# Graph attention on one core: the scores of a group's four graphs as one run over six PSUM banks, and new issue orders

## What is computed

```python
h = relu(layernorm(x))                      # over the last axis, eps 1e-5
q, k, v = h @ Wq + bq, h @ Wk + bk, h @ Wv + bv      # split into 6 heads of 64
scores = q @ k.T / sqrt(64)                 # per graph and head, 128 x 128
probs = softmax(scores + where(adj, 0, -9e15))
out = x + (concat_heads(probs @ v) @ Wf + bf)
```

## Time and profile before

| | |
|---|---|
| median of 3 runs | 470.05 us (470.0 to 470.82) |
| span of the profiled execution, first to last instruction | 468.2 us |
| own time of the profiled execution | not recorded beside the span; the median of the runs is 1.85 us above the span |
| PE busy | 459.1 us (98%) |
| DVE, ACT, POOL busy | 365.0, 361.6, 303.1 us |
| granted TensorE clock | 1.00 in every slice (the 2.4 GHz level) |

### The profile page before, as it was taken

One profiled execution on the slowest core, in us unless ns is written; L12 is line 12 of the kernel. 1 busy time (PEld: TensorE's weight loads), 2 busy tenths in 40 slices (PEclk: granted clock), 3 DMA queues, 4 the chain that ended last, 5 costly groups with the idle time before them and its releaser, 6 DMA issues.

```text
span 468.2 us, 12877 instructions
## 1 busy us (share of the span) xinstructions
PE 459.1 (98%) x4457; PEld 272.9 (58%) x4457; DVE 365.0 (78%) x742; ACT 361.6 (77%) x816; POOL 303.1 (65%) x308
## 2 busy tenths in 40 slices
PE   6999999999999999999999999999999999999986
PEld 2755656566575665646556575655656565555654
DVE  6989889849988695877869687687877957796855
ACT  3889999865987778877788787688877879687670
POOL 3378578683876765666857577368577648564574
PEclk9999999999999999999999999999999999999999
DMA  8156789879889796986959586969997787788797
GB/s 302 65 121 131 151 130 192 204 141 199 202 141 234 120 212 134 198 194 128 226 111 229 124 177 133 183 146 156 199 182 146 177 170 157 182 139 149 136 158 233
DMA packets 219615, 78.56 MB, mean 168 GB/s; under 512 B 199472, under 2 KB 219568, under 8 KB 219568
## 3 DMA queue, kind: packets, MB, share of 16 engines
q1 hardware_dynamic: 209200, 65.63, 71.5%
q10 hardware_dynamic: 10368, 12.33, 9.9%
HBM read 16.19 MB, written 12.58 MB: 61 GB/s over the span
## 4 chain that ended last, share of the span: by engine, by line
PE 88%; DVE 4%; DMA 3%; ACT 2%; SPq 1%; POOL 1%; issue 1%; ACTq 0%
PE ps_proj L1013 25%; PE ps_proj L1015 24%; PE ps_proj L1014 24%; PE ps_scores L1078 7%; PE ps_ctx L1013 2%; PE ps_ctx L1014 2%; PE ps_ctx L1015 2%; DMA ct_parts<-ctx_parts 1%; DMA pt_parts<-probs_parts 1%; DVE stats L822 1%; SPq L577 1%; ACT probs L757 1%; DMA x_sb<-in_x 1%; DVE w_rows L926 1%; ACT h_pairs L730 1%
## 5 line engine op out<-in xcount | busy, mean ns | idle before, releaser
L657 POOL TENSOR_TENSOR probs_parts<-probs,probs_parts 128x768 f16<-128x768 f32 x64 | 105.2, 1648 | 39.9 <-ACT probs_parts L772 39.8
L757 ACT ACTIVATE probs<-masked,neg_max 128x128 f32<-128x128 f32 x384 | 118.2, 389 | 14.4 <-DVE neg_max L885 8.2
L1015 PE MATMUL ps_proj<-ht_parts,w_lo 128*128 128x512 f16 (+1 forms) x309 | 109.6, 360 | 0.0
L1014 PE MATMUL ps_proj<-ht_parts,w_hi 128*128 128x512 f16 (+1 forms) x309 | 109.6, 360 | 0.0
L1013 PE MATMUL ps_proj<-ht_parts,w_hi 128*128 128x512 f16 (+1 forms) x309 | 109.6, 360 | 0.0
L857 DVE SCALAR_TENSOR_TENSOR qkt_lo<-ps_proj,bias_qk,qkt_hi 128x512 f16<-128x512 f32 x94 | 68.5, 742 | 27.8 <-ACT qkt_hi L741 27.8
L741 ACT ACTIVATE qkt_hi<-ps_proj,bias_qk 128x512 f16<-128x512 f32 x94 | 62.7, 679 | 34.2 <-PE ps_proj L1015 33.9
L663 POOL TENSOR_TENSOR ctx_parts<-ctx_sb,ctx_parts 128x384 f16<-128x384 f32 x62 | 56.7, 918 | 49.9 <-ACT ctx_parts L778 49.9
L876 DVE SCALAR_TENSOR_TENSOR masked<-ps_scores,score_unscale,mask 128x384 f32<-128x384 f32 x128 | 72.0, 609 | 10.3 <-PE ps_scores L1078 9.5
L642 POOL TENSOR_TENSOR h_pairs<-h_sb,h_pairs 128x384 f16<-128x384 f32 x60 | 54.3, 916 | 37.1 <-ACT h_sb L732 36.9
L652 POOL TENSOR_TENSOR x_bf<-x_sb,b_out 128x384 f32<-128x384 f32 x64 | 63.1, 1001 | 9.6 <-DVE y_sb L908 8.1
(11 more groups left out here) (113 smaller groups left out, 916.6 us busy)
## 6 DMA issues: line engine op xcount, KB each, us to landing
x_sb<-in_x ACTq DMA_DIRECT2D x56, 192.0 KB, 3.0
y<-y_sb SPq DMA_DIRECT2D x56, 192.0 KB, 2.5
x_sb<-in_x SPq DMA_DIRECT2D x8, 192.0 KB, 5.1
y<-x_bf SPq DMA_DIRECT2D x8, 192.0 KB, 3.3
pt_parts<-probs_parts SPq DMA_TRANSPOSE x64, 4.0
ct_parts<-ctx_parts SPq DMA_TRANSPOSE x62, 2.8
adj_sb<-in_adj ACTq DMA_DIRECT2D x14, 64.0 KB, 3.6
w_raw<-in_Wk SPq DMA_DIRECT2D x1, 576.0 KB, 5.1
```

Of the source, the lines that this page charges most:

```text
L657: nc.gpsimd.tensor_tensor(probs_parts[b][:, 1, :], probs[b % 2][:], probs_parts[b][:, 0, :], ALU.subtract).then_inc(probs_split, 1)
L757: last = nc.scalar.activation(probs[b % 2][:, u * N:(u + 1) * N], masked[b % 2][:, u, :], ACT.Exp, bias=neg_max[b % 2][:, u:u + 1])
L1014: nc.tensor.matmul(to, a_hi, b_lo, start=False, stop=False)
L1015: return nc.tensor.matmul(to, a_lo, b_hi, start=False, stop=last)
```

## The change

- One PSUM tensor of eight banks without owners. Scores use banks 0 to 5 and `project_qk` the same six, in the order 0, 3, 1, 4, 2, 5; `project_v`, `weigh_values` and `project_out` use banks 6 and 7 (with exceptions in groups 0, 2, 13, 14 and 15). A table `USES_BEFORE` finds for each use who used the bank before, and PE waits for that reader.
- `scores` has three parts of four slots (24 matmuls each) in place of two runs; all four graphs' scores fit at once. A part frees its two banks when the graph after it has been masked: part 0 when `mask_scores(g,1)` is done.
- `masked`, `neg_max` and `probs` have four buffers; the exponentials are written over `masked`.
- All turns are new.

```diff
+BANK = {
+    "project_qk": (0, 3, 1, 4, 2, 5), "project_v": (6, 7, 6, 7), "project_out": (6, 7, 6, 7),
+    "weigh_values": (6, 7, 6, 7),
+}
...
+SCORE_PARTS = SCORE_BANKS // HALVES
+SCORE_SLOTS = B * K // SCORE_PARTS
+LAST_PART = (0, 1, 2, 2)
...
             def exponentials(g, b, i):
                 act.wait_ge(max_ready, nth(B, g, b, i))
-                if g >= 1 or b >= 2:
-                    act.wait_ge(probs_split, nth(B, g, b - 2, i))
                 for u in range(HEADS):
-                    last = nc.scalar.activation(probs[b % 2][:, u * N:(u + 1) * N], masked[b % 2][:, u, :], ACT.Exp,
-                                                bias=neg_max[b % 2][:, u:u + 1])
+                    last = nc.scalar.activation(masked[b][:, u, :], masked[b][:, u, :], ACT.Exp,
+                                                bias=neg_max[b][:, u:u + 1])
...
             def mask_scores(g, b, i):
-                dve.wait_ge(scores_ready, nth(2, g, b // 2, i))
+                dve.wait_ge(scores_ready, nth(SCORE_PARTS, g, LAST_PART[b], i))
...
             def free_bank(stage, group, item, i):
-                before = bank_before(stage, group, item)
-                if before is not None:
-                    was, of, at = before
+                for was, of, at in USES_BEFORE[stage, group, item]:
...
+                    if was == "weigh_values":
+                        pe.wait_ge(ctx_normalized, nth(B, of, at, i))
+                    if was == "scores":
+                        pe.wait_ge(scores_masked, nth(B, of, at + 1, i))
...
-            def scores(g, pair, i):
-                if pair == 0:
+            def scores(g, part, i):
+                if part == 0:
                     pe.wait_ge(qk_split, nth(QK, g, QK - 1, i))
-                if g == 0 and pair == 0:
-                    pe.wait_ge(v_split, 1)
-                if g >= 1 or pair >= 1:
-                    pe.wait_ge(scores_masked, nth(B, g, 2 * pair - 1, i))
+                free_bank("scores", g, part, i)
                 hi, lo = qkt_hi[g % 2], qkt_lo[g % 2]
-                for n, heads in enumerate(SCORE_PAIRS):
-                    if n == MIDDLE_BY_UPPER:
-                        pe.wait_ge(lower_done, nth(2, g, pair, i))
+                for n in range(SCORE_SLOTS):
```

More of the change, by code:

```diff
@@ L44 @@
 TURNS = {
[L45 to L62, removed]
+    "scores": (0, 10, 20), "project_v": (30, 60, 70, 90), "project_out": (10130, 10150, 10190, 20040),
@@ new lines @@
+    "project_qk": (-9950, -9920, -9890, -9860, -9830, -9820), "weigh_values": (160, 200, 10100, 10120),
+    "mask_scores": (0, 30, 40, 90), "normalize_ctx": (250, 10010, 10180, 10200), "largest_score": (20, 70, 80, 120),
+    "finish": (10230, 10240, 10310, 20050), "values_lo": (60, 100, 110, 160),
+    "statistics": (-29730, -29680, -19870, -19850), "additive_mask": (-19860,),
+    "qk_lo": (-9830, -9790, -9740, -9720, -9710, -9700), "aggregate": (-19810,), "shift": (-19780,),
+    "exponentials": (0, 60, 110, 160), "load": (-29790, -29720, -19990, -19930),
@@ L66 @@
     0: {
[L67 to L72, removed]
@@ L187 @@
[L187 to L190 removed]
+        "project_qk": (-9950, -9930, -9900, -9870, -9830, -9820), "project_v": (-9750, -9740, -9710, -9700),
+        "scores": (-9790, -9780, -9770), "weigh_values": (-9620, -9550, -9510, -9460),
@@ new lines @@
+        "project_out": (-9450, -9410, -9390, -9340), "qk_lo": (-9860, -9760, -9750, -9740, -9730, -9720),
+        "values_lo": (-9610, -9600, -9550, -9530), "mask_scores": (-9690, -9680, -9640, -9630),
+        "largest_score": (-9670, -9650, -9620, -9450), "normalize_ctx": (-9430, -9340, -9250, -9170),
+        "finish": (-9140, -9070, -9030, -9000), "qk_hi": (-9940, -9820, -9760, -9750, -9740, -9730),
+        "values_hi": (-9650, -9640, -9610, -9590), "exponentials": (-9710, -9700, -9620, -9430),
@@ new lines @@
+        "project_v": (-39170, -39120, -39110, -38960), "scores": (-39160, -39150, -39140),
+        "weigh_values": (-39020, -39000, -38930, -38880), "project_out": (-38890, -38840, -38830, -38790),
+        "statistics": (-39230, -39220, -39210, -39200), "aggregate": (-39180,), "additive_mask": (-38890,),
+        "qk_lo": (-38810, -38800, -38770, -38740, -38730, -38720), "shift": (-39110,),
+        "values_lo": (-38700, -38630, -38620, -38430), "mask_scores": (-38690, -38660, -38640, -38600),
@@ new lines @@
+        "project_v": (-48910, -48870, -48860, -48810), "scores": (-48970, -48940, -48920),
+        "weigh_values": (-48850, -48820, -48800, -48770), "project_out": (-48760, -48740, -48730, -48720),
+        "turn_ctx": (-48780, -48750), "statistics": (-48960, -48950, -48910, -48900), "aggregate": (-48860,),
+        "additive_mask": (-48750,), "qk_lo": (-48580, -48550, -48540, -48530, -48490, -48470), "shift": (-48840,),
+        "values_lo": (-48330, -48300, -48250, -48240), "mask_scores": (-48450, -48410, -48380, -48360),
```

479 lines of the change are left out of this document (247 added, 232 removed).

## The result

The changed kernel takes **495.12 us** (median of 4 runs, 493.62 to 496.5) against 470.44: ratio 1.0519, 95% interval 1.0491 to 1.0547, 24.7 us slower. The profiled execution took 496.5 us with a span of 494.5. I had forecast 474.7, range 467.0 to 480.5: the side is right, the size is not.

What follows compares the result with a forecast made beforehand. PE, busy 98% of the span, was taken as the bound: 468.2 - 2.3 - 1.6 + 3.6 + 1.9 + 2.6 + 0.5 = 472.9 us of span; with 1.85 from span to median, 474.7 us, range 467.0 to 480.5.

Steps and rivals of the forecast that it cites:

- no other place at which PE would wait by more than 0.2: Groups other than the priced loop starts and groups 3, 10 and 12: no further PE wait above 0.2 us.
- One run of scores, 2.3 less: Edges of score runs on PE: 20 runs instead of 32, each saving 0.19 us of gaps, 2.3 us less.
- rival E: Waits ahead of each score part empty PE's array: 48 gaps in place of 20, 5.3 us more; chance 0.06.
- Banks and buffers, 0: Extra semaphore waits for banks and the exponentials' dropped buffer wait: 0 us; from above 10 us, thought far off.
- The end, 1.6 less: After the last project_qk: PE's waits with lost overlap fall from 2.6 to 1.0 us, 1.6 us less.
- The loop, 3.6 more: Starts of groups 5 to 10: late x loads stall PE on bank 0, 0.6 us six times, 3.6 us more.
- L = 2.9: Assumed landing time in us of a load of x, bounds 2.3 to 3.5; PE stalls L - 2.3 per loop start.
- Group 10, 1.9; group 3, 2.6; group 12, 0.5: Late loads delay values_lo in these three groups, so PE stalls: 1.9, 2.6 and 0.5 us more.
- The period in the loop, 28.4: Time per group in the loop: 28.0 - 0.2 + 0.6 = 28.4 us, with statistics waiting for x_sb some 8 times.
- The start, 0 within 0.5: Start of the kernel: same chain through the weights, reordered, 0 us, ends -0.5 and +0.5.
- Rival D, thin margins, 0.06: DVE's margins of 0.3 to 0.5 us ahead of PE in the loop fail: 5.5 us more, 480 us; chance 0.06.
- The Trainium skill: DMA rule, 2.0 us fixed plus bytes at 436 GB/s: 192 KB load 2.45 us, stalls 3.3, time 469.4 us.

Runs made afterwards that it cites:

- all loads early: Changed kernel with 24 of ACT's entries moved, only loads of x and the mask, each to about where its buffer comes free: 482.2 us, ratio 1.0251.
- one load earlier: Changed kernel with load(G+2,1) moved from behind qk_hi(G,5) to ahead of the group's last normalize: 488.57 us, ratio 1.0399.
- the head's entries alone: Changed kernel with 17 entries of ACT and DVE moved, ahead of or around the first scores: 494.92 us.
- fillers in the changed kernel: Changed kernel with the last block of filler matmuls moved behind turn_first(0,0) and raised from 3 to 10: 491.81 us, ratio 1.0444.
- two experiments: Changed kernel with loads of x and mask moved earlier, 482.2 us; changed kernel with loads of x into a spare tile, DVE not waiting, 482.76 us.
- lists redone: Changed kernel with PE's list kept and 420 entries of the lists of ACT, DVE, POOL and SP moved: 474.67 us, ratio 1.0071.

## Why the prediction was wrong

**The step that failed** is "I went through the other groups in the same way and found no other place at which PE would wait by more than 0.2", and with it "At the start I see the same chain through the weights, reordered: 0". The changed kernel's timeline has 14 more gaps of 0.4 to 2.5 us between 60 and 465 us, 13.9 us together, and 3.7 us in the head. Against the forecast span of 472.9, the measured 494.5 is 21.6 more, and the terms add up to 22.1: 13.9 at places that I had put at nothing, 3.7 in the head, 4.0 more than forecast at the starts in the loop, about 1 by which the waits behind 465 us shrank less than forecast, minus 0.5 at the three places that I had named. I had traced loads to the waits of DVE right behind them and stopped there. One example of how waits go on, ACT and then PE, ahead of `scores(4)`:

```profile
127.43 0.71 ACT L749 ACTIVATE h_pairs<-x_sb,shift_by,rstd 128x384 f16<-128x384 f32 x1 [4.44 <-DVE shift_by L855]
...
130.41 1.61 ACTq L734 DMA_DIRECT2D x_sb<-in_x  x1
132.07 1.27 ACT L760 ACTIVATE qkt_hi<-ps,bias_qk 128x512 f16<-128x512 f32 x2 [1.17 <-issue]
```

```profile
138.28 0.23 PE L1102 MATMUL ps<-qkt_hi 64*128 64x128 f16 x2 [2.03 <-DVE qkt_lo L874]
```

The late mask of group 5 holds DVE for 1.9 us ahead of the statistics, `shift` comes behind these, and `normalize(5,0)` waits 4.4 us on ACT, with `load(6,0)`, `load(6,1)` and `qk_hi(4,2)` to `(4,5)` behind it; the scores need the last of these. The late transfer has a part in a wait of PE two engines further on, in another group's work. It isn't the whole of this one. With the mask early ACT still waits 3.5 us there (the run with all loads early). And of the 2.0 us of PE's wait above, 1.3 belong to this one execution: the start of a load took 1.61 us on ACT's queue in place of 0.34, and ACT idled 1.2 us. In the runs with one load earlier, with the head's entries alone and with fillers in the changed kernel, whose lists are the same at this place, PE waited 0.7 to 0.8 us:

```profile
137.43 0.23 PE L1107 MATMUL ps<-qkt_hi 64*128 64x128 f16 x2 [0.75 <-DVE qkt_lo L879]
```

Point by point:

- *One run of scores, 2.3 less.* Right: the gaps at the scores' edges sum to 6.1 us before and to 3.7 after, and none lies between parts (rival E is out). In the loop, with its load early, PE loses 0.9 against 2.1 before.
- *Banks and buffers, 0.* Right for the buffers (measured 0). For the banks no wait is seen that a set semaphore makes.
- *The end, 1.6 less.* Wrong. The ledger's last stretch shows 1.0 less, but it leaves out a wait that stands 1.2 us of work ahead of it. From the last `project_qk` on, which is how I had bounded this term, PE's waits with their overlap are 2.6 us before and 3.0 after, 0.4 more. I had found 0.4 for the last probabilities and 0.6 for the last two contexts; the longest waits for a transpose of each kind are 0.76 and 1.09:

```profile
465.50 0.20 PE L1040 MATMUL ps<-v_hi,pt_parts 128*128 128x65 f16 x1 [0.76 <-DMA pt_parts<-probs_parts]
...
486.96 0.34 PE L1040 MATMUL ps<-w_hi,ct_parts 128*128 128x384 f16 x1 [1.09 <-DMA ct_parts<-ctx_parts]
```

- *The loop, 3.6 more.* Mechanism right, size off: 7.6 us of gaps over six starts, nearly all back when the load was moved. The term was L = 2.9; at 227.85 it was 3.6, for which the prediction's own L - 2.3 gives 1.3 a start, 7.8 in all. The gaps fall to 1.1 a start in the later rounds. I missed that the first to stall is `project_out`, on bank 7.
- *Group 10, 1.9; group 3, 2.6; group 12, 0.5.* 1.80 at 324.91, 1.65 at 122.30 and 1.06 at 393.51, all for `v_lo`. Right places, 4.5 in place of 5.0.
- *The period in the loop, 28.4.* 28.9 us, and 29.5 and 29.8 between its first starts. Statistics wait 15 times for x_sb, where I gave some 8.
- *The start, 0 within 0.5.* Wrong: 3.7 us in the ledger of the profiled run. Fillers there gave 3.3 us in the timed runs, though the profiled head with them lost 17.6 against 18.3.
- *Rival D, thin margins, 0.06.* This had the better part of the truth, in kind: waits for `qkt_lo`, `v_lo`, transposes. But it was priced in the loop, where there are none; they lie in the groups ahead of it and behind it.
- *The Trainium skill*, "DMA: Bandwidth & Descriptors", section "Anatomy of one DMA", gives the 2.0 us and the 436 GB/s from which I had the estimate of 2.45 us, but it gives them for DMAs that GpSimd starts, and these loads are started from ACT's queue; I had left that out. The loads of the changed kernel landed at a median of 3.1, and 3.6 at the place that counts, later than the estimate. Going by rows was right, only not far enough.

Of 24.7 us: 12.9 are late loads (two experiments agree). About 2 to 3 are the missing fillers (measured 3.3 alone, 2.1 beside early loads). The other 9 or so lie in the order of the lists of ACT, DVE, POOL and SP, since moving their entries brought nearly all of them back with PE's order kept; 5.2 of these went with the loads and their starts. That they are margins at which a transfer of usual or slightly longer landing reaches PE is my reading. Which entries carry them was not told apart one by one.

## What to carry to other kernels

- When every engine works through a fixed list, follow a late transfer through each list that it touches, to the end: DVE's wait here held ACT's next entries, and these held PE in another group. The check of the entries right behind the wait found 12 of the 26 us of gaps between 60 and 465 us.
- Price a transfer at the place where it counts, with what else is in flight there, and ask of a new order how much later a transfer may land before PE notices. Kernels with the same new order on PE ranged from 469.5 to 495.1 us here, by the lists of the other engines and a few fillers.
- What a small edit gains where it is made can be lost again within 20 us, as with the head's entries; look at the ledger, not at the one wait.
- Before a wait of one trace is explained, look for it in the traces of kernels with the same lists there. One wait of 2.0 us was 0.7 to 0.8 in three others.

## What the runs showed of the hardware

- An idle PE can cost more than the idle time. Seven profiled executions have one gap of 2.6 to 2.9 us without matmuls in the head. In five of them the granted clock was 0.50 to 0.72 in the window from 12 to 15 us, and in two, the changed kernel and the one with the head's entries alone, it stayed at 1.00. The gap isn't the only way to it: it was 0.54 from 9 to 12 us in the run with the exponentials in place, where no gap of the head is over 1.1 us, at no cost in time (470.21 us). In the five profiled runs with fillers there the clock stayed at 1.00 through the head.
- A load started from ACT's queue held that queue for 0.34 us in the median of 56, and for 1.61 us once, with ACT idle for 1.2 us behind it.
- Single transfers landed late outside the loop. In the run with lists redone, from 200 to 280 us:

```profile
x_sb<-in_x ACTq DMA_DIRECT2D x12, 192.0 KB, 2.8
...
pt_parts<-probs_parts SPq DMA_TRANSPOSE x12, 3.8
```

and from 314 to 328 us, behind the loop:

```profile
q8 instruction: 1, 0.02, 0.5%
...
x_sb<-in_x ACTq DMA_DIRECT2D x1, 192.0 KB, 6.0
...
pt_parts<-probs_parts SPq DMA_TRANSPOSE x2, 5.3
```

These few transfers are not the rule: over all of 330 to 440 us the medians are 3.0 for x_sb and 3.8 for the transposes of probabilities, near those of the loop, and over 30 to 160 us 3.1 and 4.4. The queues of kind "instruction" move data in most stretches of 10 us outside the loop and in none from 190 to 290 us of that run. That the one causes the other was not tested.
